# State-space stage: part of the last doubling of twelve power tables is computed by ScalarE and finished on VectorE

## The reference, cut to what matters

```
dtA = dt[:, None] * A
dC = C * (exp(dtA) - 1.0) / A
powers = exp(dtA[:, :, None] * arange(L))
K = 2.0 * einsum('dn,dnl->dl', dC, powers).real
y = irfft(rfft(x, n=2 * L) * rfft(K, n=2 * L))[:, :L] + x * D_skip
```

## Time and profile before

| what | value |
| --- | --- |
| median of 3 runs | 3926.74 us (3923.39 to 3928.51) |
| profiled execution, span from first to last instruction | 3923.9 us |
| share of the span busy | PE 81%, DVE 76%, ACT 58%, POOL 40% |
| state-space stage within the span | about 1989 to 2494 us |
| mean granted TensorE clock over the span | 0.890 |

### The profile page before, as it was taken

One profiled execution on the slowest core, in us unless ns is written; L12 is line 12 of the kernel. 1 busy time (PEld: TensorE's weight loads), 2 busy tenths in 40 slices (PEclk: granted clock), 3 DMA queues, 4 the chain that ended last, 5 costly groups with the idle time before them and its releaser, 6 DMA issues. The chain is left out here.

```text
span 3923.9 us, 54505 instructions
## 1 busy us (share of the span) xinstructions
PE 3188.6 (81%) x17202; PEld 2121.8 (54%) x17202; DVE 2978.2 (76%) x7467; ACT 2267.9 (58%) x2921; POOL 1587.3 (40%) x1268
## 2 busy tenths in 40 slices
PE   7638768777887587877987787689999999958999
PEld 3314334444443344445865555477777777746776
DVE  7799999999999999986679998434444334469888
ACT  4579678888987788882133333133323232347876
POOL 0025556555555466555500000113332323217775
PEclk9868878888888788878999999899999999989999
DMA  8710000000000000002223333643444442330212
GB/s 318 260 42 10 10 8 10 10 12 10 10 10 10 8 10 10 12 5 90 93 54 90 83 93 83 188 129 124 129 131 129 129 129 89 113 119 15 62 54 69
DMA packets 262025, 290.53 MB, mean 74 GB/s; under 512 B 53264, under 2 KB 175782, under 8 KB 260588
## 3 DMA queue, kind: packets, MB, share of 16 engines
q1 hardware_dynamic: 243964, 259.49, 21.9%
q10 hardware_dynamic: 14736, 12.89, 1.0%
q0 software_dynamic: 3040, 14.94, 1.0%
HBM read 218.82 MB, written 68.45 MB: 73 GB/s over the span
## 5 line engine op out<-in xcount | busy, mean ns | idle before, releaser
L1119 PE MATMUL up<-ctx,attnT 128*128 128x384 f32 (+1 forms) x1664 | 717.2, 587 | 45.5 <-ACT attnT L989 45.5
L1089 PE MATMUL score<-KT,q 64*128 64x512 f32 (+1 forms) x1792 | 380.2, 518 | 336.9 <-ACT S L949 246.2
L850 DVE MAX8 both_wide<-S 128x8 f32<-128x146 f32 (+1 forms) x2816 | 601.2, 295 | 44.0 <-ACT S L949 24.7
L809 POOL TENSOR_TENSOR S<-S 128x512 f32<-128x512 f32 (+1 forms) x224 | 424.6, 1928 | 355.1 <-DVE S L855 355.1
L1119 PEld LDWEIGHTS up<-ctx,attnT 128*128 128x128 f32 (+1 forms) x1664 | 366.1, 231 | 322.0 <-issue 162.5
L855 DVE SCALAR_TENSOR_TENSOR S<-S,both_wide 128x3202 f32<-128x3202 f32 x128 | 472.8, 3757 | 14.6 <-ACT both_wide L980 14.6
L1089 PEld LDWEIGHTS score<-KT,q 64*128 64x128 f32 x1792 | 172.3, 235 | 535.1 <-ACT S L949 399.9
L949 ACT ACTIVATE S<-score 128x1024 f32<-128x1024 f32 (+1 forms) x448 | 402.7, 931 | 90.3 <-PE score L1089 90.0
L2242 DVE TENSOR_TENSOR ff_gelu<-ff_whole,ff_gelu 128x512 fp32r<-128x512 f32 x128 | 100.5, 785 | 426.6 <-ACT ff_gelu L2436 426.6
L958 ACT ACTIVATE both_wide<-S,below 128x3202 bf16<-128x3202 f32 x128 | 379.7, 2967 | 43.3 <-DVE below L890 22.5
L980 ACT ACTIVATE both_wide<-S,ebias 128x3202 f32<-128x3202 f32 x128 | 376.3, 2964 | 23.9 <-DVE S L855 13.5
(11 more groups left out here) (435 smaller groups left out, 5982.4 us busy)
## 6 DMA issues: line engine op xcount, KB each, us to landing
s_hankel<-scratch_K SPq DMA_DIRECT2D x128, 256.0 KB, 4.4
ff_w_low<-scratch_w1l SPq DMA_DIRECT2D x112, 256.0 KB, 2.6
ff_w_low<-scratch_w2l SPq DMA_DIRECT2D x112, 256.0 KB, 2.7
xt_prep<-in_x SPq DMA_DIRECT2D x8, 1024.0 KB, 8.5
scratch_xt<-xt_prep SPq DMA_DIRECT2D x8, 1024.0 KB, 8.1
both_wide<-in_ffn_w_t POOLq DMA_DIRECT2D x8, 1024.0 KB, 11.0
q<-scratch_qt SPq DMA_DIRECT2D x128, 64.0 KB, 1.9
mod_xt<-in_x_turned SPq DMA_DIRECT2D x32, 256.0 KB, 2.6
```

The source lines that it names most:

```text
L809: nc.gpsimd.tensor_tensor(S[:, b, 0, chunk(j)], S[:, b, 0, chunk(j)], S[:, b, 1, chunk(j)], ALU.add).then_inc(s["summed01"], 1)
L850: nc.vector.max(cand[:, h, 8 * k:8 * k + 8], S[:, b, h, k * SEG:min((k + 1) * SEG, G)])
L1089: last = nc.tensor.matmul(score[bank(p, j)][:, e, 0:w], lhsT=q[at, b, part, h // 2, :], rhs=KT[at, h // 2, chunk(j)], start=(part == 0), s ...
L1119: last = nc.tensor.matmul(up[:, 0:DV], lhsT=attnT[0:w, e, c - 4 * g, :], rhs=ctx[0:w, c, :], start=(c == 0), stop=(c == GC - 1))
```

## The change

For tables 4 to 15 (SPLIT_FROM = 4) the last doubling is divided by pairs. Pairs 8 to 15 (`rest`) are done on VectorE as before, but with 8 pairs and 32 powers in an instruction, so that one round of four products (512 elements) and four sums (256) does it. For pairs 0 to 7 (CROSSED = 8) ScalarE writes the crosswise products into the upper half of the table: real part <- minus imaginary factor times imaginary part, imaginary part <- imaginary factor times real part, 16 activations of 64 elements, each with its factor as a per-partition operand (`cross(g)`). VectorE then waits for `crossed` and adds the real factor times the lower half by 8 fused steps (scalar_tensor_tensor) of 128 elements. The negated imaginary factors are made once by GpSimd at the stage's start (`minus_W`). In ScalarE's order the crossing of an even table g + 1 stands in gather g, ahead of copy j = 6 (CROSS_AT); that of an odd table g + 3 stands behind spread g.

```diff
@@ -1444,12 +1444,17 @@
     BLOCK = POWERS
     BLOCKS = CHUNKS // BLOCK
     BOTH = 2 * GP
+    CROSSED = GP // 2
+    HALF = 1 << LEVELS - 1
+    SPLIT_FROM = 4
+    CROSS_AT = 6
     with scope:
         Q = first_tables + [sb(f"s4_Q{k}", [P, 2, GP, P + 1]) for k in range(2, RING)]
         S = sb("s4_S", [P, 2, 2, CHUNKS + 1, BOTH])
         QT = sb("s4_QT", [P, 2, 4, P])
         M = sb("s4_M", [P, 2, 2, 2, GP, PIECE])
         R = M.rearrange("p a b c k w -> p (a b c k w)")
+        M_wide = M.rearrange("p a b c k w -> p a b c (k w)").rearrange("p a b c (k w) -> p a b c k w", w=2 * PIECE)
         turn = sb("s4_turn", [P, BLOCK, 2, 2, BOTH])
         hankel = sb("s4_hankel", [P, LOADS, SIDE, P])
         yT = sb("s4_yT", [P, 4, P])
@@ -1458,6 +1463,7 @@
         Kz = sb("s4_Kz", [P, 2, ROWS, CHUNKS * SIDE + 2])
         Krow = sb("s4_Krow", [P, KROW])
         skip = sb("s4_skip", [P, PARTS])
+        minus_W = sb("s4_minus_W", [P, PARTS, CROSSED])
         tp = [ps(f"s4_tp{k}", [P, 4, P]) for k in range(2)]
         utp = ps("s4_utp", [P, 2, 2, P])
         stp = ps("s4_stp", [P, 2, 2, P])
@@ -1466,7 +1472,7 @@
         ksp = ps("s4_ksp", [P, P])
         x_by_channel = X[:].rearrange("p c d -> p (c d)").rearrange("p (d c) -> p d c", c=CHUNKS)
         s = {n: sem("s4_" + n) for n in (
-            "skip_in", "row_set", "Kz_ready", "Q_ready", "turned", "QT_ready", "U_done", "UT_ready", "U_turned", "U_copied", "turn_ready",
+            "skip_in", "row_set", "Kz_ready", "minus_W_ready", "Q_low", "crossed", "Q_ready", "turned", "QT_ready", "U_done", "UT_ready", "U_turned", "U_copied", "turn_ready",
             "K_done", "K_row", "K_stored", "h_in0", "h_in1", "h_in2", "h_in3", "h_used", "S_ready", "y_done", "yT_ready", "y_turned",
             "y_copied", "y_stored")}
         YG = PART // OUT
@@ -1558,6 +1564,7 @@
                         last = nc.gpsimd.tensor_scalar(to[:, :, 0, 1], source[:, :, 1, both(G)], -1.0, None, ALU.mult)
                     last.then_inc(s["turn_ready"], 1)
 
+                nc.gpsimd.tensor_scalar(minus_W[:], W[:, LEVELS - 1, 1].rearrange("p (g k) -> p g k", k=GP)[:, :, 0:CROSSED], -1.0, None, ALU.mult).then_inc(s["minus_W_ready"], 1)
                 pool.drain()
                 kernel_weights(0)
                 chunk_turn(0)
@@ -1596,7 +1603,8 @@
                     dve.drain()
                     sums(P, 1, 1)
                     sums(1, 1, 0)
-                    for level in range(1, LEVELS):
+                    split = g >= SPLIT_FROM
+                    for level in range(1, LEVELS - 1 if split else LEVELS):
                         n = 1 << level
                         for first in range(0, n, 2 * PIECE):
                             dve.drain()
@@ -1605,6 +1613,27 @@
                             dve.drain()
                             for slot in range(min(2, -(-n // PIECE))):
                                 last = sums(n + first + slot * PIECE, min(n, PIECE), slot)
+                    if not split:
+                        last.then_inc(s["Q_ready"], 1)
+                        return
+                    last.then_inc(s["Q_low"], 1)
+                    w = 2 * PIECE
+                    rest = slice(CROSSED, GP)
+                    of = slice(GP * g + CROSSED, GP * (g + 1))
+                    dve.drain()
+                    for slot in range(2):
+                        for part in range(2):
+                            v.tensor_tensor(M_wide[:, slot, part], Q[b][:, :, rest, w * slot:w * (slot + 1)],
+                                            W[:, LEVELS - 1, part, of].unsqueeze(1).unsqueeze(3).broadcast_to([P, 2, GP - CROSSED, w]), ALU.mult)
+                    dve.drain()
+                    for slot in range(2):
+                        to = slice(HALF + w * slot, HALF + w * (slot + 1))
+                        v.tensor_tensor(Q[b][:, 0, rest, to], M_wide[:, slot, 0, 0], M_wide[:, slot, 1, 1], ALU.subtract)
+                        v.tensor_tensor(Q[b][:, 1, rest, to], M_wide[:, slot, 0, 1], M_wide[:, slot, 1, 0], ALU.add)
+                    dve.wait_ge(s["crossed"], g - SPLIT_FROM + 1)
+                    for k in range(CROSSED):
+                        last = v.scalar_tensor_tensor(Q[b][:, :, k, HALF:P], Q[b][:, :, k, 0:HALF], W[:, LEVELS - 1, 0, GP * g + k:GP * g + k + 1],
+                                                      Q[b][:, :, k, HALF:P], ALU.mult, ALU.add)
                     last.then_inc(s["Q_ready"], 1)
 
                 def carry(first, halves):
@@ -1698,9 +1727,19 @@
                                                     scale=-1.0 if part else 1.0)
                     last.then_inc(s["U_copied"], 1)
 
+                def cross(g):
+
+                    act.wait_ge(s["Q_low"], g - SPLIT_FROM + 1)
+                    for k in range(CROSSED):
+                        for part, factor in ((0, minus_W[:, g, k:k + 1]), (1, W[:, LEVELS - 1, 1, GP * g + k:GP * g + k + 1])):
+                            last = nc.scalar.activation(Q[g % RING][:, part, k, HALF:P], Q[g % RING][:, 1 - part, k, 0:HALF], ACT.Copy, scale=factor)
+                    last.then_inc(s["crossed"], 1)
+
                 def gather(g):
 
                     for j in range(TG):
+                        if j == CROSS_AT and g % 2 and SPLIT_FROM <= g + 1 < PARTS:
+                            cross(g + 1)
                         act.wait_ge(s["turned"], TG * g + j + 1)
                         nc.scalar.activation(QT[:, j % 2], tp[j % 2][:], ACT.Copy).then_inc(s["QT_ready"], 1)
                         if j % 4 == 1 and j > 4:
@@ -1733,10 +1772,13 @@
                             nc.scalar.activation(y[:, :, first:first + OUT], yp[:].rearrange("p d c -> p c d"), ACT.Copy).then_inc(s["y_copied"], 1)
 
                 gather(0)
+                act.wait_ge(s["minus_W_ready"], 1)
                 gather(1)
                 for g in range(PARTS - 2):
                     gather(g + 2)
                     spread(g)
+                    if g % 2 == 0 and SPLIT_FROM <= g + 3 < PARTS:
+                        cross(g + 3)
                 spread(PARTS - 2)
                 spread(PARTS - 1)
                 act.wait_ge(s["y_copied"], YG * PARTS)
```

## The result

The changed kernel takes 3947.62 us (median of 5 runs, 3946.95 to 3949.77), against 3926.74 us before (5 runs, 3923.39 to 3928.51): ratio 1.0054, 95% interval 1.0042 to 1.0065, so slower by about 21 us, or half a per cent. The profiled execution's span is 3945.8 us.

What follows compares the result with a forecast made beforehand. VectorE bounds the kernel now, with 4.65 us of slack to the TensorE chain ScalarE copies for, which then decides. Start +5.4 and five periods +17 make +22.4 us on 3926.7: 3949 us, range 3928 to 3965.

Steps and rivals of the forecast that it cites:

- The bound: State-space stage: VectorE sets today's period; the gather and spread chain ScalarE copies for has 4.65 us slack, then decides.
- ScalarE's price: Crosswise products on ScalarE: 0.243 us per 64-element activation, 3.9 us for the sixteen of a table.
- The cheap crossing: Rival on ScalarE's crossings: 0.10 to 0.15 us per activation, slack just used up, 3925 to 3931 us; chance 0.10.
- The fused steps: VectorE's last doubling: eight fused steps of 128 elements take 2.2 us, cutting its work by 1.85 us a table.
- The stall inside the odd gathers: Even tables' crossing ahead of copy 6: gather 9 loses 1.75 us, as does every later step of TensorE's chain.
- The odd crossing: Behind spread 8: VectorE idles some 4 us before the fused steps; a period grows 3.4 us, five periods 17 us.
- The start: First split tables, 4 and 5: gather 3 stalls 7.5 us, a half clock follows, table 5 ends 5.4 us later.
- The sum: Whole kernel: start 5.4 plus periods 17 gives +22.4 us on the median of 3926.7, so 3949 us.
- the last part: From the end of table 15 on: no crossing, the old work, only later.
- the longest gap is 0.16 us: Reading of VectorE's row through table 10, the carry and table 11: the longest gap is 0.16 us.
- VectorE stays the bound: Rival: odd crossing is done when VectorE's own half is; periods of 59.2 us, 3909.5 us in all; chance 0.13.
- The clock falls once more: Rival: the 1.75 us stall in gather 9 brings another half clock, 2.15 us a period, +11, 3960 us; chance 0.15.

Runs made afterwards that it cites:

- dve_alone: The change without the crossings' activations and their waits, leaving VectorE's new last doubling alone; 3908.0 us against 3926.4 for the kernel before, ratio 0.9951.
- gpsimd_scalar: The change with crosswise products made by GpSimd in 16 tensor_scalar instructions of 64 elements a table; 3961.86 us against 3925.94 for the kernel before, ratio 1.0089.
- mid_spread_odd: The change with only odd tables split and their crossing inside the spread, ahead of ScalarE's second copy; 3911.42 us, ratio 0.9960 to the kernel before.
- odd_only: The change with only odd tables (5 to 15) split, their crossings still behind the spreads; 3936.18 us against 3926.4 for the kernel before, ratio 1.0026.
- the first run: The change with crosswise products made by GpSimd in two tensor_tensor instructions of 512 elements a table; 3921.39 us against 3925.25 for the kernel before, ratio 0.9988.
- The second: The GpSimd version with 16 tensor_scalar instructions of 64 elements a table instead of two tensor_tensor; 3961.86 us against 3925.94 for the kernel before, ratio 1.0089.

## Why the prediction was right

The forecast was 3949 us, the measurement 3947.6. Point by point:

- *The bound.* The chain that ScalarE copies for did become the bound: in all five periods the odd table ends 6.05 to 6.09 us after the last copy of the spread (forecast 4.1 + 2.2 = 6.3), whenever that copy ends, and TensorE's wait for the table is 6.74 to 6.75 us each time. Moving the odd crossing out of this place took the loss back.
- *ScalarE's price*, taken at 0.243 us from a row of twice the size: 0.240 measured. The cheap crossing is refuted by this line alone.
- *The fused steps*: 2.19 us for eight, taken at 2.2 from the row; the estimate of 1.55 us by the Trainium skill (VectorE: DVE Perf Modes, "The TRN2 errata") does not hold here; the measurement decides.
- *The stall inside the odd gathers*, 1.75 us: its state copies end 20.2 us after the period's start (2280.61 + 1.06 - 2261.45) against 18.76 before, so 1.45. Mis-sized by 0.3, mostly since the low part is there after 11.0 us rather than 11.2. The carry waits 3.00 us, as said.
- *The odd crossing*: the fused steps wait 3.6 to 6.4 us, forecast about 4 (the 6.36 us is the period with the half clock in its spread); TensorE waits 6.75 us before the gathers, forecast about 7; periods 65.6 on average, forecast 65.3. That is closer than the terms are. The stall is 1.4 us on average and the end 6.07, together some 0.6 less than forecast, while the chain from the state copies to the last copy takes 39.3 us against 38.5, a growth that the forecast had at nothing. Half of the 0.85 us comes from the one period with the half clock in its spread; the rest is not explained. So the match of the periods is in part luck.
- *The start*: 4.8 us against 5.4. The product held up in gather 3 starts 7.6 us later than before (each counted from the stage's start), forecast 7.5. Only 5.5 us of it are idle time on TensorE's row, since TensorE came to this point 1.9 us late, after a half clock at the end of spread 1. A half clock follows (1.07 us for eight products that take 0.63).
- *The sum*: start 4.8 and periods 18.3 make 23.1, forecast 22.4, while the runs show 20.9 and the spans 21.9. The difference lies in the last part, from table 15's end to the start of the last copy: 59.0 us against 61.0, where the forecast had "the old work, only later". Nothing shows that the change shortened it. In the eleven traces this part takes 58.9 to 61.4 us, and 61.4 both without any crossing on ScalarE (dve_alone) and in the slowest kernel (gpsimd_scalar). Of the 2.0 us, 1.4 are a half clock that the kernel before has in this part and the changed one hasn't (last section). That the total fits to 1.4 us is thus luck by about 2 us.
- *A misreading*: "the longest gap is 0.16 us" is not so. At 2289.93 VectorE stands idle for 0.43 us inside table 11, without a releaser; no term of the sum uses it.
- *VectorE stays the bound* was to be decided by whether the odd crossing ends by the time of VectorE's own half. It didn't in the change, and did in mid_spread_odd, which then runs at 60 us a period.
- *The clock falls once more*: not where I had put it. The stalls of 1.0 to 1.4 us in the odd gathers were followed by full speed in all five. It fell in one spread (2249.66).

## What to carry to other kernels

Before handing work to an engine with a low busy share, find the spot in its queue at which the input is there and nothing that decides waits behind it, and hold the time of the work against the slack of that spot. The split costs 21 us with its crossings inside a gather and behind a spread; for the odd tables alone, with the crossing in the spread's own 5 us gap, it gains 14. When a step ahead of a wait for another chain gets faster (here the even tables, ahead of the carry), it gains little: all twelve tables with nothing on ScalarE (dve_alone, 3908 us) are only 3 us ahead of the six odd ones.

## What the runs showed of the hardware

A short wait of TensorE can be followed by the half clock. A transfer wait of 1.76 us in the changed kernel is followed by sixteen matmuls in 1.08 us instead of 0.67, where I had expected 2.3 us to be harmless by the earlier trace rows. TensorE's timeline of odd_only has it after 1.30 and 1.22 us:

```profile
2210.35 0.52 PE L1864 MATMUL s_ytp<-s_hankel,X 128*32 128x128 f32 x8 [1.30 <-DMA s_hankel<-scratch_K]
2210.80 1.08 PE L1870 MATMUL s_ytp<-both_wide,s_S 64*32 64x128 f32 x16
...
2274.92 0.43 PE L1864 MATMUL s_ytp<-s_hankel,X 128*32 128x128 f32 x8 [1.22 <-DMA s_hankel<-scratch_K]
2275.28 1.07 PE L1870 MATMUL s_ytp<-s_Q,s_S 64*32 64x128 f32 x16
```

These are the two periods of 64.5 and 65.0 us (mean granted clock 0.90 and 0.89, against 0.93 in those of 63.4 and 63.7). The fifth, of 66.0 us, has the same after a wait of 1.43 us (clock 0.89). So the excess over the forecast of 63.5 lies in the periods with such a fall. The kernel before has one too, behind its last table; the changed kernel, at the same place and after nearly the same wait, hasn't:

```profile
2455.75 0.43 PE L1822 MATMUL s_ytp<-s_hankel,X 128*32 128x128 f32 x8 [1.18 <-DMA s_hankel<-scratch_K]
2456.10 0.93 PE L1828 MATMUL s_ytp<-both_wide,s_S 64*32 64x128 f32 x16
```

```profile
2480.86 0.42 PE L1864 MATMUL s_ytp<-s_hankel,X 128*32 128x128 f32 x8 [1.16 <-DMA s_hankel<-scratch_K]
2481.21 0.67 PE L1870 MATMUL s_ytp<-both_wide,s_S 64*32 64x128 f32 x16
```

A wait of 2.13 us in the kernel before (2488.62) left the clock at full as well. So the length of the wait alone doesn't decide; what does stays open.

VectorE and GpSimd hold each other up when both read tables: VectorE loses 1.7 us beside 2.5 us of GpSimd's two-tensor work, or GpSimd takes 1.5 us for an instruction that takes 0.44 alone. The Trainium skill has a rule for it (SBUF — State Buffer, "SBUF: two separate sides": the two share a port pair, and a VectorE instruction with two SBUF inputs or a GpSimd instruction holds it as an exclusive lock for the whole instruction). It ought to have been in my expectation of the first run, which fits it. The second fits in that GpSimd waits, but VectorE loses only 0.04 us there (2.54 against 2.50) beside GpSimd's first two instructions, less than the 0.4 us that one of these takes alone, which the rule as the page has it doesn't explain. The two runs differ in the number of tensors, in the size and in the operation, so which of them decides who waits is not shown.
